# Attention in four column tiles of 32, with the output turned by VectorE out of PSUM

## The reference

```python
score = jax.nn.softmax(jnp.einsum('bihd,bjhd->bhij', q, k), axis=-1)
v = _lin(xn, Wv, bv).reshape(b, n, R, HD)                 # R = 8 rules, HD = 8
out = jnp.einsum('bhij,bjrd->bihrd', score, v)
qv = _lin(xn, Wqv, bqv).reshape(b, n, H, 1, QK) / np.sqrt(QK)
comp = jnp.concatenate([broadcast(qv), out], axis=-1) @ Ws.T + bs
comp = jax.nn.softmax(comp, axis=3)                       # over the rules
out = (comp * out).sum(axis=3).reshape(b, n, DIM)
out = res + _lin(out, Wf, bf)
return out + _lin(relu(_lin(_ln(out), Wr1, br1)), Wr2, br2)
```

## Time and profile before

| | us |
|---|---|
| median of three runs | 1222.99 |
| span of the profiled execution | 1220.2 |
| PE busy in it | 1168.7 (96%) |
| DVE busy | 951.7 (78%) |
| POOL busy | 956.5 (78%) |
| ACT busy | 756.2 (62%) |
| mean granted clock of TensorE | 0.985 |
| an along group (514.56 to 579.80) | 65.24 |
| a plain group (903.77 to 967.19) | 63.42 |

### The profile page before, as it was taken

How to read it: one execution, slowest core, us unless ns; L and a number is a source line. 1 busy time by engine, 2 the same in 40 slices (tenths; PEclk the granted TensorE clock), 3 DMA queues, 4 the chain that set the end, 5 groups by cost and what they waited for, 6 DMA issues and landing times.

```text
span 1220.2 us, 27563 instructions
## 1 busy us (share of the span) xinstructions
PE 1168.7 (96%) x7997; PEld 541.7 (44%) x7997; DVE 951.7 (78%) x2127; ACT 756.2 (62%) x1461; POOL 956.5 (78%) x561
## 2 busy tenths in 40 slices
PE   4699999999999999999999999999999999997898
PEld 2144444444444444444444444444444444435675
DVE  7676788888888787878788888788888878768762
ACT  4066766666666766666666676666666666664443
POOL 5277898989898898988898989898888878883321
PEclk9599999999999999999999999999999999999999
DMA  5334444344444443444444344544344434330000
GB/s 128 109 66 92 100 96 106 79 107 97 110 90 100 94 94 84 101 101 90 100 96 105 84 105 95 111 98 98 85 92 93 93 83 98 73 71 18 18 26 26
DMA packets 55765, 107.14 MB, mean 88 GB/s; under 512 B 6144, under 2 KB 25056, under 8 KB 55728
## 3 DMA queue, kind: packets, MB, share of 16 engines
q0 software_dynamic: 18784, 67.70, 29.3%
q1 hardware_dynamic: 36162, 38.65, 10.1%
q10 hardware_dynamic: 782, 0.33, 0.1%
HBM read 22.51 MB, written 8.39 MB: 25 GB/s over the span
## 4 chain that ended last, share of the span: by engine, by line
PE 83%; DVE 8%; issue 4%; DMA 2%; POOL 1%; ACT 1%; DVEq 1%; SPq 0%; POOLq 0%; ACTq 0%
PE out_bank L1077 33%; PE row_bank L1048 17%; PE col_bank L1067 17%; PE den_bank L917 5%; DVE rowmax L1242 3%; PE turn_bank L926 2%; PE down_bank L1501 2%; DVE att_all L389 2%; DMA q_op<-max_rows 1%; PE turn_bank L254 1%; PE mid_bank L1521 1%; PE den_bank L934 1%; POOL norm_rstd L576 1%; DVE norm_normed L584 0%; PE out_bank L1491 0%
## 5 line engine op out<-in xcount | busy, mean ns | idle before, releaser
L1242 DVE TENSOR_REDUCE rowmax<-row_bank 128x1 f32<-128x512 f32 x1024 | 662.7, 685 | 184.5 <-PE row_bank L1048 180.3
L1192 ACT ACTIVATE prob<-col_bank 128x512 f32<-128x512 f32 x1024 | 554.7, 594 | 263.6 <-PE col_bank L1067 261.9
L1077 PE MATMUL out_bank<-prob,v_op 128*64 128x512 f32 x2048 | 534.4, 594 | 0.2 <-ACT prob L1192 0.2
L1351 POOL TENSOR_TENSOR addend<-prob 128x1024 f32<-128x1024 f32 x128 | 323.4, 2526 | 45.6 <-ACT prob L1192 45.6
L1351 POOL TENSOR_TENSOR quad<-prob 128x1024 f32<-128x1024 f32 x128 | 335.5, 2621 | 20.4 <-ACT prob L1192 20.2
L1048 PE MATMUL row_bank<-k_op,q_op 72*64 72x512 bf16 x2048 | 327.0, 387 | 13.5 <-DMA q_op<-q_parts 9.0
L1067 PE MATMUL col_bank<-q_op,k_op 74*64 74x512 bf16 x2048 | 317.2, 382 | 3.1 <-DMA q_op<-max_rows 2.0
L1067 PEld LDWEIGHTS col_bank<-q_op,k_op 74*64 74x64 bf16 x2048 | 118.1, 109 | 246.2 <-ACT prob L1192 208.3
L1048 PEld LDWEIGHTS row_bank<-k_op,q_op 72*64 72x64 bf16 x2048 | 122.6, 109 | 153.4 <-DVE rowmax L1242 55.2
L1077 PEld LDWEIGHTS out_bank<-prob,v_op 128*64 128x64 f32 x2048 | 152.9, 136 | 67.3 <-issue 8.3
L1356 POOL DMA_DIRECT2D quad<-addend x128 | 112.7, 880 | 77.5 <-POOL addend L1351 72.9
(11 more groups left out here) (201 smaller groups left out, 805.9 us busy)
## 6 DMA issues: line engine op xcount, KB each, us to landing
quad<-addend POOLq DMA_DIRECT2D x128, 512.0 KB, 5.3
k_op<-k_parts SPq DMA_DIRECT2D x64, 144.0 KB
q_op<-q_parts SPq DMA_DIRECT2D x192, 48.0 KB
v_op<-v_all SPq DMA_DIRECT2D x32, 256.0 KB, 5.9
q_parts<-along_parts SPq DMA_DIRECT2D x11, 192.0 KB, 2.1
k_parts<-along_parts SPq DMA_DIRECT2D x33, 64.0 KB, 2.1
out<-y_out SPq DMA_DIRECT2D x8, 256.0 KB, 2.3
q_op<-max_rows SPq DMA_DIRECT2D x64, 4.0 KB
```

What stands on the lines that cost most here:

```text
L1077: last = nc.tensor.matmul(out_bank[ih * VW:(ih + 1) * VW, :], v_op[slot // 2][:, t, :], outs.halves(prob[:, t, :])[:, :, ih, :], start=(t ...
L1192: nc.scalar.activation(prob[:, t, h * HALF:(h + 1) * HALF], col_bank[h][:, :], ACT.Exp).then_inc(exp_done, 1)
L1242: nc.vector.tensor_reduce(rowmax[:, parity, t, h:h + 1], row_bank[h][:, :], AX.X, ALU.max).then_inc(max_done, 1)
L1351: pool.tensor_tensor(dst, prob[:, 2 * k, :], prob[:, 2 * k + 1, :], ALU.add).then_inc(pair_done, 1)
```

## The change

- Scores, values and projections go in four column tiles of 32 (`QUARTERS`). A score bank is filled by four matmuls of 32x512; the values of a tile by eight of 32x256: two halves of the 64 value columns, each in four tiles that hold a quarter of the queries. The denominators of a unit become eight matmuls of 32x256, accumulated over k.
- With that layout a transpose of each 32x32 block puts the output straight into the rows of `mix_in`. DVE does it out of PSUM, one instruction of 128x512 for each unit at t = 1 of the next slot, ahead of the row maxes. The denominators are transposed the same way (128x256) in place of the reduction in the mixing step.
- `turn_out` and `turn_den` leave PE; `take_out`, `take_turned` and `take_den` leave ACT.
- `out_bank` is doubled, by the parity of the slot; `turn_bank` is gone, and what it served (turn of the row maxima, projections) uses the `out_bank` not in use. PE waits for the transposed output of the unit before ahead of these.
- `project.qk` moves from (2,2) to (2,3), `project.values` from (3,0) to (3,2), and what takes their results moves with them.
- DVE's loops are written out for two groups, since the bank depends on parity. In the last group and the feed-forward part the banks are renamed, and the turn of the last unit's output is one transpose on DVE.

```diff
@@ PE: scores
-                    for c in range(2):
-                        last = nc.tensor.matmul(row_bank[h][c * VW:(c + 1) * VW, :],
-                                                q_op[slot][0:PROD_ROWS, t * P + c * VW:t * P + (c + 1) * VW],
+                    for e in QUARTERS:
+                        last = nc.tensor.matmul(row_bank[h][e, :],
+                                                q_op[slot][0:PROD_ROWS, t * P + e.start:t * P + e.stop],
...
@@ PE: values, denominators (class Outputs)
+    def quarter(self, t, q):
+        return t.rearrange("p (e q i) -> p q e i", q=P // QT, i=QT)[:, q]
+    def values(self, pe, slot, v, prob, t):
+        bank = self.out_bank[slot % 2]
+        for half in range(VW // QT):
+            for q, rows in enumerate(QUARTERS):
+                last = self.nc.tensor.matmul(bank[rows, half * QCOLS:(half + 1) * QCOLS],
+                                             v[:, t, half * QT:(half + 1) * QT], self.quarter(prob, q),
+                                             start=(t == 0 and half == 0), stop=(t == TB - 1), skip_group_check=True)
...
-        for ih in range(2):
-            for k in range(2):
-                q = 32 * (2 * ih + k)
-                last = self.nc.tensor.matmul(self.den_bank[q:q + 32, :], self.onehot[:, slot, :],
-                                             self.halves(self.quad[:, QUAD_SET[slot], k, :])[:, :, ih, :],
+        for k in range(2):
+            for q, rows in enumerate(QUARTERS):
+                last = self.nc.tensor.matmul(self.den_bank[rows, 0:QCOLS], self.onehot[:, slot, :],
+                                             self.quarter(self.quad[:, QUAD_SET[slot], k, :], q),
...
-    def turn_out(self, pe, u):
...
+    def turn_out(self, dve, u, parity, slot):
+        dve.wait_ge(self.pv_done, TB * u + TB)
+        self.nc.vector.transpose(
+            self.mix.mix_in[:, parity, :, slot, :].rearrange("p e (h r) -> p h e r", r=QT),
+            self.out_bank[slot % 2][:, :].rearrange("p (h e i) -> p h e i", h=VW // QT, i=QT)).then_inc(
+                self.mix.mix_in_ready, 1)
@@ DVE: denominators of the mixing
-            dve.wait_ge(self.den_turned, G + 1)
-            sums = self.den_bank[:, :].rearrange("p (e k s) -> p e s k", k=2, s=32)[:, :, 0:SLOTS, :]
-            self.nc.vector.tensor_reduce(self.den[:, :, :], sums, AX.X, ALU.add).then_inc(self.den_ready, 1)
+            dve.wait_ge(self.den_done, SLOTS * G + SLOTS)
+            self.nc.vector.transpose(self.den[:, :, :].rearrange("p e s -> p (e s)"),
+                                     self.den_bank[:, 0:QCOLS]).then_inc(self.den_ready, 1)
@@ PE: a group
-                            elif not (first and s < 2):
-                                pe.wait_ge(mix_in_ready, u - 1)
+                            if not (first and s == 0):
+                                pe.wait_ge(mix_in_ready, u)
                             turn_max(u + 1, (s + 1) % 2)
...
-                            outs.turn_out(pe, u - 1)
-                            if s == 1 and not first:
-                                outs.turn_den(pe, G - 1)
...
-                        if along and (s, t) == (2, 2):
-                            pe.wait_ge(mix_in_ready, u - 1)
+                        if along and (s, t) == (2, 3):
+                            pe.wait_ge(mix_in_ready, u)
                             project.qk(pe, G)
-                        if along and (s, t) == (3, 0):
-                            pe.wait_ge(mix_in_ready, u - 1)
+                        if along and (s, t) == (3, 2):
+                            pe.wait_ge(mix_in_ready, u)
                             project.values(pe, G)
@@ DVE: a group
+                        if t == 1 and before:
+                            outs.turn_out(dve, u - 1, parity if s > 0 else 1 - parity, (s - 1) % SLOTS)
                         for h in range(2):
                             if not (last and av >= SLOTS):
                                 row_max(u - s + av, av % 2, tv, h)
...
-            with dve.Fori(1, PAIRS_ALONG) as G:
-                group(G, False, False, True)
+            with dve.Fori(0, (PAIRS_ALONG - 1) // 2) as H:
+                group(H * 2 + 1, 1, False, False, True)
+                group(H * 2 + 2, 0, False, False, True)
```

More of the change, by code:

```diff
@@ L41 @@
 COLUMN_TILES = (slice(0, P // 2), slice(P // 2, P))
+QT = 32
+QUARTERS = tuple(slice(q, q + QT) for q in range(0, P, QT))
+QCOLS = TB * QT
 HALF = SEQ // 2
@@ L252, in qk @@
         for m in range(2):
-            for e in COLUMN_TILES:
+            for e in self.tiles:
                 last = self.nc.tensor.matmul(self.qk_bank[self.bank_at(n)][e, m * PAIR_COLS:(m + 1) * PAIR_COLS],
@@ L1065, in col_scores @@
                         pe.wait_ge(exp_done, 2 * TB * u + 2 * t + h - 1)
-                    for c in range(2):
-                        last = nc.tensor.matmul(col_bank[h][c * VW:(c + 1) * VW, :],
-                                                k_op[slot][0:ROWS, t * P + c * VW:t * P + (c + 1) * VW],
+                    for e in QUARTERS:
+                        last = nc.tensor.matmul(col_bank[h][e, :],
+                                                k_op[slot][0:ROWS, t * P + e.start:t * P + e.stop],
                                                 q_op[slot][0:ROWS, h * HALF:(h + 1) * HALF],
@@ L1075, in values @@
                 pe.wait_ge(exp_done, 2 * TB * u + 2 * t + 2)
-                for ih in range(2):
-                    last = nc.tensor.matmul(out_bank[ih * VW:(ih + 1) * VW, :], v_op[slot // 2][:, t, :],
-                                            outs.halves(prob[:, t, :])[:, :, ih, :], start=(t == 0), stop=(t == TB - 1))
-                last.then_inc(pv_done, 1)
+                outs.values(pe, slot, v_op[slot // 2], prob[:, t, :], t)
             def group(G, first, last, along):
@@ L1218, in group @@
                             joined.take(act, 0, logit_bank)
-                        if along and (s, t) == (2, 3):
+                        if along and (s, t) == (2, 4):
                             for m in range(2):
@@ L1276, in _, with group @@
             }
-            def group(G, first, last, along):
+            def group(G, parity, first, last, along):
                 for s in range(SLOTS):
```

110 lines of the change are left out of this document (30 added, 80 removed).

## The result

The changed kernel takes 1255.11 us (median of 4 runs, 1252.31 to 1259.68) against 1222.55 for the kernel before: a ratio of 1.0257, interval 1.0225 to 1.0289. It is **slower by 2.6%**; 1207 was forecast, with a range from 1190 to 1232.

The account below looks back on a forecast made before the run. PE was taken to bound the loop. Ten along groups gave -8.0, four plain -4.8, group 0 -2.0 and the last -1.2, together -16.0 from 1223: 1207 us, range 1190 to 1232.

Parts of the forecast that it names:

- The turns leave PE: PE, tile 6 of each slot: turns of output and denominators go, PE works 3.5 us a group less.
- Four tiles at no cost: PE, scores, values, denominators, projections: four column tiles of 32 run side by side as two do; no change in PE's time.
- The transpose at 0.6 a piece: DVE, one 128x512 fp32 transpose out of PSUM per unit: 0.6 us each, priced from the row max.
- The second rival: DVE's transpose costs two passes, 1.2 to 1.3 us, adding 2.2 a group: 1241, slower than before; chance 0.10.
- DVE's lateness: PE waits for DVE around the ends of slots 3 and 1 and early in slot 3: 3.3 us a group, 0.56 already there.
- The sum without jumps: PE works 3.5 us less and waits 2.7 to 2.8 more: -0.8 an along group; a plain one -1.2.
- POOL's floor: Along groups: removing POOL's waits of 1.6 us from 65.24 leaves 63.6, below which a group can't become much shorter.
- The first rival: PE's longer loop no longer stays loaded; each jump back fetches code, about 1 us net, twelve back edges: 1219; chance 0.26.
- The third rival: Row maxes reach the next slot's operand too late by DMA; PE waits 1.4 us in one slot a group: 1229; chance 0.12.

Follow-up runs that it names:

- the best kernel: Changed kernel with PE's and DVE's loops written out whole and slot 0's first accumulating DMA issued after the third pair sum: 1198.88 us, ratio 0.9797.

## Why the prediction was wrong, point by point

- **The turns leave PE, 3.5 a group.** Right. Tile 6 is 1.73 in slots 1 and 3 and 3.46 in 0 and 2.
- **Four tiles at no cost.** Right for the change as it is, with a period of 1.73; the reason given was too thin. What counts is that all operations have one size: mixtures of 32 and 64 cost some 0.26 a tile, which the prediction had not weighed.
- **The transpose at 0.6 a piece.** Right: 708 ns busy, against 685 for a row max. The second rival falls (by its own terms it would have decided from 0.9 a transpose on, not from 0.95; nothing hangs on that). Its estimate from the Trainium skill ("VectorE: DVE Perf Modes", section "The three transpose paths"), four times 311 ns, a figure for bf16, disagrees with the trace by 0.53 us; the measurement decides.
- **DVE's lateness, 3.3 a group.** Nearly right. In the best kernel, where nothing else disturbs, tile 0 of slot 0 is 1.40 over the period (1.36 forecast), tiles 0 to 2 of slot 2 are 0.76 + 0.48 + 0.39 = 1.63 over it (1.45 forecast), and slot 3's tiles 1 and 2 are not late (0.5 forecast). That lateness adds up fully, as the second rival's price supposed, is wrong: a third of an added transpose reached PE.
- **The sum without jumps: -0.8 an along group, -1.2 a plain one.** In the best kernel 63.84 and 62.1 stand against 65.24 and 63.42: -1.4 and -1.3, close to POOL's floor of 63.6. The two terms, turns less lateness, held in kind, and the along group gave 0.6 more than forecast. But that kernel is not the one predicted: its loops are written out and its DMA moved. With the loops written out alone the means are 65.1 and 62.7, -0.2 and -0.7, and the whole is 1218.6. That 1198.9 lies near 1207 is therefore no support for the sum.
- **The first rival, mis-sized, is where the prediction failed.** The forecast's sum had no term for the jump; the rival named it, its 12 places and its signs, and set about 1 us net for each, "with 0 and 4 as ends". In the kernel before with longer code and the same tiles it costs 5.8. Three things were missing. The branch took 4.2 in the median of the along loop and 5.6 in the plain one, not the 2.1 of the fastest DMA. Behind the idle time the granted clock is at its lower level for 3.4 to 6.8 us at ten of the twelve jumps. And DVE's lateness covers little of it. In the changed kernel tile 7 of slot 3 and the two tiles behind it take 10.8 at the nine along jumps (5.41, 2.61, 2.73) and 13.2 at the three plain ones; in the best kernel, which does not jump, the three take 6.6, of which 1.4 is DVE's lateness. So a jump is 4.2 and 6.6 more than no jump there, 57 us for all twelve, and the two profiled executions are 61 apart. The Trainium skill ("Runtime: NRT & Kernel Launch", section "Instruction fetch mechanics") spoke for this rival and the trace agrees that the branch waits; that page of the Trainium skill gives PE room for 2048 instructions, but passes of 1777 wait here and those of 1543 do not. The chance of 0.26 was too low for a rule with no row against it.
- **An edit costed at nothing: DVE's loop of two groups.** It waits for code as well, 2.2 us at every second along group; with PE's jumps gone, writing this loop out took 10.4 us off. The prediction did not look at it.
- **The third rival was taken as an alternative, and it adds.** With the jumps gone, waits for the row maxes' DMA were worth 19.7 us, near the 22 that were worked out; in the kernel as changed they are 3.0 us and mostly hidden by the jumps, as it seems: they grow to 7.5 without PE's jumps and to 12.0 without either engine's. The forecast left them out because DVE's lateness at the same place would cover them; they stand at slot 1, where DVE is not late and an accumulating DMA of slot 0 is ahead. That DMA is not in the same queue, as the prediction has it: q0 moves 67.70 MB, which is what POOL's 128 DMAs of 512 KB come to, and SP's go by another.
- Working back: 1255.1 to 1229.0 by PE's jumps, to 1218.6 by DVE's, to 1198.9 by the DMA. The order matters, since each hides a part of the next: PE's 26.1 is only 2.2 a jump, most likely because DVE's jump and the DMA's wait came out behind it, as the 57 us above say.

## What to carry to other kernels

A change that splits matmuls multiplies an engine's instructions: count those of a loop's pass, for every engine whose loop is written out further, and treat the jump back as a full stop most often with a stretch at the lower clock behind it, unless a pass of that length is known to stay loaded; here, writing the loops out whole removed it, as code that runs straight on is read ahead at no cost. Use one column-tile size for all matmuls that follow each other. Rivals that fall on different places add up: take them together in the range, and where one is removed, look for the wait behind it.

## What was not expected of the hardware

- A change between column tiles of 64 and 32 costs PE 0.11 to 0.14 us each time, at the full clock.
- Passes of 1031 and 1543 instructions on PE stay loaded; 1777, 1853, 1863, 2289, 2365, 2567 and 4727 don't. On DVE 205 stay, and 366 and 426 don't. PE's jump back then takes 3.3 to 5.9 us, also where the pass is but little too long; on DVE the wait behind it is 1.5 to 2.3 us.
- After 3.5 us in which PE stood still, its clock fell to 1.2 GHz only when work came again, and stayed there for 3.4 us in the case shown; behind other jumps of the same kernel it was up to 6.8, and behind two of them it did not fall.
- An addition of 128x32 on DVE took 4.05 us on average (0.19 to 5.0) beside POOL's additions, where a reciprocal at the same place takes 0.35; in the case shown it ends with POOL's. The Trainium skill ("SBUF — State Buffer", section "SBUF: two separate sides") has a pair of ports that DVE and POOL lock against each other, DVE for operations with two SBUF inputs or in a two-port mode among them. The rows fit that, but no run here tested it.
